# One warp, four feed-forward layers, one core: the written-out issue order of the four compute engines is replaced

## The reference, cut to what matters

```python
x = x + L0_ffn(rigid_transform(x, dx, angle))        # bilinear warp; 1.58-bit FFN, gelu
x = x + L1_ffn(masked_attention_pool(x, types))      # 4 experts of 256-1024-256, top 2 of 4
x = x + L2_ffn(language_adapter(x, language_ids))    # 64-wide adapter, layernorm; 256x256 product
x = x + L3_ffn(category_matrix(x, cat_ids))          # one 256x256 matrix per image; gated FFN, silu
```

## Time and profile before

| quantity | value |
|---|---|
| median of 3 runs | 3265.25 us (3265.25 to 3265.64) |
| the profiled execution | 3265.25 us, span 3263.0 us |
| mean granted TensorE clock | 0.889 of full speed |
| TensorE busy (matmul) | 2813.0 us, 86% |
| VectorE busy | 1916.6 us, 59% |
| ScalarE busy | 1667.7 us, 51% |
| GpSimd busy | 1460.8 us, 45% |

### The profile page before, as it was taken

The page is one execution under the profiler, slowest core; times in us unless marked ns, Lnnn a source line. Parts: engine busy times, 40 slices in busy tenths (PEclk is TensorE's granted clock), DMA queues, the critical chain, the costliest instruction groups (busy, mean ns, idle before and its releaser), DMA issues.

```text
span 3263.0 us, 53348 instructions
## 1 busy us (share of the span) xinstructions
PE 2813.0 (86%) x14652; PEld 2241.1 (69%) x14652; DVE 1916.6 (59%) x5747; ACT 1667.7 (51%) x2786; POOL 1460.8 (45%) x1796
## 2 busy tenths in 40 slices
PE   3028999999999999999999999999999999999996
PEld 2017777777787777777877777777777777877784
DVE  5355765656566556556665665666656565665432
ACT  0024655555565555556645555565555555655442
POOL 0476554445455544444554444445544454551100
PEclk9558998989999898989989898999989899999996
DMA  4222222211222222212222221222222212221110
GB/s 190 59 39 64 55 61 58 57 44 41 58 56 56 59 58 58 44 42 54 58 58 58 58 52 37 56 54 56 61 57 57 45 41 59 54 55 44 41 38 7
DMA packets 207651, 179.37 MB, mean 55 GB/s; under 512 B 122959, under 2 KB 164692, under 8 KB 206164
## 3 DMA queue, kind: packets, MB, share of 16 engines
q1 hardware_dynamic: 172084, 123.84, 14.0%
q0 software_dynamic: 32768, 39.91, 6.7%
q10 hardware_dynamic: 2466, 11.75, 0.9%
HBM read 156.98 MB, written 9.99 MB: 51 GB/s over the span
## 4 chain that ended last, share of the span: by engine, by line
PE 75%; SPq 9%; DVE 3%; issue 3%; POOL 2%; DMA 2%; ACT 2%; ACTq 0%; DVEq 0%; POOLq 0%
PE bank L1211 27%; PE bank L1222 24%; SPq L528 9%; PE bank L1114 5%; PE bank L1120 4%; PE bank L1102 2%; PE bank L1275 2%; POOL w_win L888 2%; PE bank L1108 2%; PE bank L1251 2%; PE bank L1262 2%; DMA c<-w_out 2%; PE bank L1243 1%; PE bank L1163 1%; PE bank L1178 1%
## 5 line engine op out<-in xcount | busy, mean ns | idle before, releaser
L888 POOL DMA_INDIRECT w_win<-in_windows,w_idx x1024 | 1071.4, 1046 | 412.2 <-issue 295.5
L1211 PE MATMUL bank<-c_T,moe_w 128*128 128x256 f32 x4096 | 1045.5, 401 | 0.0
L1222 PE MATMUL bank<-moe_w,moe_hidden_T 128*128 128x256 f32 x4096 | 976.4, 381 | 0.3 <-ACT moe_hidden_T L1042 0.3
L1211 PEld LDWEIGHTS bank<-c_T,moe_w 128*128 128x128 f32 x4096 | 810.2, 202 | 136.7 <-issue 23.8
L1222 PEld LDWEIGHTS bank<-moe_w,moe_hidden_T 128*128 128x128 f32 x4096 | 758.5, 190 | 125.5 <-issue 21.9
L1042 ACT ACTIVATE moe_hidden_T<-bank,moe_b 128x256 f32<-128x256 f32 x1024 | 428.5, 470 | 404.2 <-PE bank L1211 402.6
L640 DVE TENSOR_TENSOR w_prod<-w_win,w_hat 128x72 f32<-128x72 f32 x2048 | 327.2, 229 | 131.5 <-issue 131.2
L895 POOL TENSOR_SCALAR front_stats<-front_stats 128x2 f32<-128x2 f32 x32 | 6.1, 192 | 843.8 <-ACT q_front L980 843.7
L790 DVE SCALAR_TENSOR_TENSOR x_back<-bank,gates,x_back 128x256 f32<-128x256 f32 x256 | 112.0, 479 | 272.8 <-PE bank L1222 272.6
L1243 PE MATMUL bank<-xT_back,adapters 128*64 128x64 f32 x512 | 85.0, 318 | 177.3 <-ACT xT_back L1048 177.3
L1243 PEld LDWEIGHTS bank<-xT_back,adapters 128*64 128x64 f32 x512 | 61.7, 208 | 204.4 <-issue 161.5
(11 more groups left out here) (222 smaller groups left out, 4123.3 us busy)
## 6 DMA issues: line engine op xcount, KB each, us to landing
L_cond_W<-in_L_cond_W SPq DMA_DIRECT2D x128, 256.0 KB, 3.3
adapters<-in_adapter SPq DMA_DIRECT2D x128, 224.0 KB
w_win<-in_windows,w_idx POOLq DMA_INDIRECT x1024
gamma_beta<-in_gamma_beta SPq DMA_DIRECT2D x128, 128.0 KB
moe_w<-in_moe_w ACTq DMA_DIRECT2D x2, 4096.0 KB
x_front<-in_x SPq DMA_DIRECT2D x32, 256.0 KB
c<-w_out SPq DMA_DIRECT2D x512, 16.0 KB
L_cond_b<-in_L_cond_b SPq DMA_DIRECT2D x128, 64.0 KB, 3.0
```

The costliest lines, as they stand in the source:

```text
L888: gp.indirect_dma_start(out=V[par][:, g_ * WLEN:(g_ + 1) * WLEN], out_offset=None, in_=t["windows"], in_offset=bass.IndirectOffsetOnAxis(a ...
L1211: last = te.matmul((H0, H1)[j % 2][:, (i % 2) * QT:(i % 2 + 1) * QT], moe1[:, (e * NDB + d) * F + f * P:(e * NDB + d) * F + (f + 1) * P], ...
L1222: last = te.matmul(Y[:, u * D:(u + 1) * D], hT[:, (i % 4) * QT + u * P:(i % 4) * QT + (u + 1) * P], moe2[:, i * D:(i + 1) * D], start=(f = ...
```

## The change

Only the table `SLOT` changes: no instruction is added or removed, and no semaphore, buffer or DMA. The order in which the four engines issue the steps of a turn is another one. SP's order stays. `coords` moves from VectorE's slot 0 to 28, `hats` to the last four slots of ScalarE, the steps of all other stages are spread anew.

```diff
--- before.py
+++ after.py
@@ -86,32 +86,33 @@
 
 SLOT = {
     "vector": {
-        "coords": (0,),
-        "front": (1, 2, 3, 4, 5, 6, 7, 8, 15, 18, 20, 22, 23, 24, 25, 26, 28, 37, 39, 40, 41, 42, 43, 44, 52, 53, 54,
-                  67, 68, 69, 70, 74, 75, 76, 89, 91, 92, 93, 95, 96, 98, 99, 100, 101, 102, 104, 105, 107),
-        "warp": (9, 10, 11, 21, 29, 33, 45, 56, 57, 58, 59, 62, 63, 64, 65, 66, 79, 80, 83, 84, 86, 87, 88, 90, 94, 97),
-        "back": (12, 13, 14, 16, 17, 19, 27, 30, 31, 32, 34, 35, 36, 46, 47, 48, 49, 50, 51, 55, 61, 71, 72, 73, 77, 78,
-                 81, 82, 103),
-        "experts": (38, 60, 85, 106),
+        "front": (0, 1, 2, 3, 4, 5, 6, 7, 11, 14, 15, 17, 18, 19, 20, 21, 24, 29, 30, 32, 33, 34, 35, 36, 46, 48, 62,
+                  63, 64, 65, 66, 71, 72, 73, 77, 78, 79, 80, 84, 92, 93, 94, 95, 96, 97, 98, 99, 107),
+        "back": (8, 9, 10, 13, 16, 22, 26, 37, 38, 39, 40, 41, 42, 47, 54, 55, 56, 57, 58, 59, 68, 82, 83, 85, 86, 87,
+                 88, 89, 106),
+        "warp": (12, 25, 27, 31, 43, 44, 45, 50, 51, 52, 53, 60, 61, 67, 69, 70, 74, 75, 76, 90, 91, 100, 101, 102, 103,
+                 104),
+        "experts": (23, 49, 81, 105),
+        "coords": (28,),
     },
     "gpsimd": {
-        "front": (0, 9, 15),
-        "gather": (1, 2, 3, 4, 5, 6, 8, 10, 11, 12, 13, 14, 17, 18, 19, 20, 21, 22, 23, 24, 25, 26, 27, 28, 29, 30, 31,
-                   32, 33, 34, 35, 36, 37),
-        "back": (7,),
-        "mask": (16,),
+        "gather": (0, 2, 3, 5, 9, 10, 11, 12, 13, 14, 15, 16, 17, 18, 19, 20, 21, 22, 23, 24, 25, 26, 27, 28, 29, 30,
+                   31, 32, 33, 34, 35, 36, 37),
+        "front": (1, 6, 8),
+        "back": (4,),
+        "mask": (7,),
     },
     "scalar": {
-        "front": (0, 4, 6, 9, 12, 13, 18, 19, 25, 27, 32, 35, 36, 42, 46),
-        "back": (1, 3, 7, 10, 14, 17, 20, 23, 26, 28, 31, 37, 38),
-        "experts": (2, 5, 8, 11, 15, 16, 21, 22, 24, 29, 30, 33, 34, 40, 41, 44),
-        "hats": (39, 43, 45, 47),
+        "front": (0, 5, 6, 10, 13, 14, 18, 21, 23, 25, 30, 32, 34, 37, 43),
+        "back": (1, 2, 11, 15, 20, 22, 24, 27, 29, 33, 36, 39, 42),
+        "experts": (3, 4, 7, 8, 9, 12, 16, 17, 19, 26, 28, 31, 35, 38, 40, 41),
+        "hats": (44, 45, 46, 47),
     },
     "tensor": {
-        "back": (0, 2, 4, 11, 13, 15, 17, 22, 24, 28, 35, 36, 42, 43, 54, 59),
-        "experts": (1, 5, 6, 8, 9, 12, 14, 16, 19, 20, 23, 25, 26, 29, 31, 32, 33, 38, 39, 40, 41, 45, 46, 47, 48, 50,
-                    52, 55, 56, 57, 58, 60, 61, 63),
-        "front": (3, 7, 10, 18, 21, 27, 30, 34, 37, 44, 49, 51, 53, 62, 64),
+        "back": (0, 2, 5, 16, 18, 21, 25, 29, 31, 35, 39, 46, 47, 52, 58, 63),
+        "experts": (1, 3, 4, 7, 9, 10, 11, 13, 14, 15, 17, 20, 23, 24, 26, 27, 28, 33, 37, 38, 41, 42, 43, 44, 45, 51,
+                    53, 54, 55, 56, 57, 59, 60, 61),
+        "front": (6, 8, 12, 19, 22, 30, 32, 34, 36, 40, 48, 49, 50, 62, 64),
     },
 }
 DVE_STEPS, POOL_STEPS, ACT_STEPS = 120, 18, 4
```

## The result

The changed kernel takes 3432.69 us in the median (3430.69 to 3447.45, 4 runs), the kernel before 3265.44 us beside it (3265.25 to 3266.69, 4 runs): a ratio of 1.0521, 95% interval 1.0492 to 1.0551. It is 167 us slower; 151 were forecast (3416 us), and 3433 lies in the range.

What follows compares the result with a forecast made beforehand. TensorE, 86% busy, bounds the kernel, idling at L1243 for the chain down block, store, regroup, b_T0. 3.77 + 1.14 + 0.9 - 0.8 = 5.0 us in 29 turns, 145, plus 6: 3265 to 3416 us; range 3345 to 3455.

Steps and rivals of the forecast that it cites:

- The second down block: TensorE slot 59 to 63: store, regroup and restart start later by two Y blocks and L1192, +3.77 us a turn.
- Context and router: TensorE slots 48 to 50, now adjacent: idle ahead of L1178 and L1186, +1.14 us a turn, bounds 0 and 1.6.
- The first gate/up pair: TensorE slot 31 waits for ScalarE's q1T, now behind the hid block's gelus: +0.9 us a turn, bounds 0 and 1.5.
- The clock: Turn start: L1251, now behind the second hid block, runs at the high clock, -0.8 us a turn, bounds 0 and -1.1.
- The prologue: Turns -1 and 0, without a store: last warp part at slot 104 instead of 97; guess 6 us, bounds 0 and 12.
- The table load: First Silu on ScalarE: the skill's drain of about 1.38 us, up to 40 us in the sum, was left out.
- Only the move counts: Rival: the copies stay hidden, leaving 3.77 - 0.8 = 3.0 us a turn, 3351 us; chance 0.12.
- no earlier rise: Rival: clock's rise keeps its distance from the restart, 5.8 us a turn, 3439 us; inside the forecast's own range, 0.64.
- the clock no longer falls: Rival: every restart runs at the high clock, -0.2 us a turn, 3259 to 3265 us; 0.06 with the no-effect rival.
- the change does nothing: Rival: the store does not hold the regroup and slot 63 costs nothing; 0.06 together with the full-clock rival.
- VectorE comes late: Rival: at the turn's end VectorE is one L643 (1.35 us) behind, 6.4 us a turn, 3456 us; chance 0.15.

Runs made afterwards that it cites:

- e3: Kernel before with only the second down block moved behind the last two Y blocks and L1192, back_out1 behind the fourth combination: 3958.24 us against 3855.00, ratio 1.0276.
- e1: Changed kernel with SP's regroup of the warp issued ahead of the store: 4242.04 us, ratio 1.0986 to the kernel before.
- e2: Kernel before with SP's regroup of the warp issued ahead of the store: 3631.74 us against 3855.00, ratio 0.9414.
- e6: Changed kernel with ScalarE's copy q1T ahead of the gelus of the hid block before it: 4438.96 us; unedited changed kernel beside it 4439.24.
- p3: p2 with expert blocks again between transpose, context and router, and q1T ahead of the gelus: 3581.52 us, ratio 1.0969 to the kernel before.
- e7: Changed kernel with the turn's start on TensorE in the old order, L1252 ahead of the second hid block: 4456.37 us; unedited changed kernel beside it 4439.24.
- p1: Kernel before with a GpSimd memset and wait behind each of a turn's last 21 gathers: 3339.73 us against 3266.51, ratio 1.0223.
- p2: Changed kernel with a GpSimd memset and wait behind each of a turn's last 29 gathers: 3550.55 us, ratio 1.0872 to the kernel before.

## Why the prediction was right, and where its sizes were off

- **The second down block.** Forecast +3.77 a turn. e3 has it alone: 3.56. In the changed kernel the chain behind it keeps its length, and the restart's wait grows as said (11.21 us where some 11.2 were forecast; the mean is 9.9, since at the loop's jump some of it lies ahead of other lines). This term carries some 60% of the loss (3.56 x 29 = 103 us of the 167), and e1 and e2 show from the other side that the store's wait is what ties the regroup to the block.
- **Context and router.** Forecast +1.14, and just outside its upper bound of 1.6: the idle times are to the digit those of the earlier trace rows, 0.46 and 0.68, but from L1173 to the next Y block it is 3.59 us in the mean, where the three groups took 1.92 between other blocks: +1.67. The rest, 0.53, is in the blocks themselves: a block ahead of a gap loses its overlap of 0.16 with the next, two times here, and the two blocks behind the gaps are 0.11 and 0.10 us longer than in the kernel before, where TensorE does not idle ahead of them (durations are modelled):

```profile
1615.77 1.05 PE L1178 MATMUL bank<-mask,x_front 128*128 128x128 f32 x8
...
1618.39 0.95 PE L1186 MATMUL bank<-router,c_T 128*128 128x4 f32 x8
```

The term of the sum was mis-sized: I added the gaps and left the overlaps out, though for the gate/up pair I had counted them.
- **The first gate/up pair.** Forecast +0.9; 28.9 us in 32 waits are 0.90 a turn. What remains of the stretch's +6.48 after 1.67 and the forecast's own 3.77 for the move is 1.04. No run separates this term: e6 was hidden by the stall, and p3 has it together with the copies.
- **The clock.** Forecast -0.8, found -0.67; e7, which undoes it, costs 17 us, 0.6 a turn.
- **The prologue.** A guess of 6 us with bounds 0 and 12; it was 12.2, at the upper bound. The trace shows where it stands, not which step of these turns holds it; no run separates it.
- **The table load.** The row was the better guide. In the changed kernel a load of 1.28 us starts at 1689.54 and its Silu at 1690.84, again 0.02 us after its end, and TensorE waits for VectorE's product (L850) 3.9 us in the whole kernel, as before. By the estimate from the drain in the Trainium skill (ScalarE: Activation LUTs, What ACT_TABLE_LOAD costs) the sum would have been up to 40 us higher; the forecast without it was 17 us too low, and the terms above are larger than that.
- **The rivals.** "Only the move counts" is refuted by the three waits, "no earlier rise" by L1252's median of 379 ns, "the clock no longer falls" by the hid block behind the restart (3.78 us), "the change does nothing" by the time. "VectorE comes late" did not happen: L864 starts 1.08 us behind the down block's start in the turn shown, as before. It was near: VectorE, done with the warp's last part, waits for the last Y block only 0.6 to 0.95 us in the turns of the loop, and one more L643 (1.35 us) would have made it late.

```profile
1629.80 0.88 DVE L791 SCALAR_TENSOR_TENSOR x_back<-bank,gates,x_back 128x256 f32<-128x256 f32 x2 [0.94 <-PE bank L1223]
```

In the sum the forecast was 5.0 us a turn and 6 of prologue; the profiled execution has 6.0 and 12. The mechanism was right and two sizes were low, the copies and the prologue, of which the second was a guess. The upper end of 3460 named with the bounds of the copies comes out of no sum of these terms: with the copies at 1.6 and 1.5 it is 3447, with the prologue at 12 as well 3453. Of the 36 us by which the profiled one lies above the forecast (3452 - 3416), 28 are the turns' missing microsecond and 6 the prologue. Against the median it is 17 too low; that the median is nearer to the forecast than the execution that was divided up is luck, and what makes the 20 us between them isn't shown.

What was wrong is a statement that the prediction did not make but invites: that each term is a price to be had back. p3 took back the copies' two terms and lost them again to VectorE and ScalarE.

**What stays open.** Why the engines stand still in the gathers in three groups and not in the others, and whether it is the chip. That the gap ends about with the run, and that it is longer with the longer run, is what the traces show; that the run causes it was to be shown by p1 and p2, and these met no stall. The kernels with each other's GpSimd table were not run. And the best order found, e2, has no time without the stall.

## What to carry to other kernels

When a transfer waits in a queue behind a store, everything that moves the store's producer later moves the transfer, whatever the transfer itself needs; look at what the queue issues next before you look at the engines. Price a chain from the instruction that starts it, and fill the time behind it with what would otherwise stand ahead. And a wait that is taken away is a gain only if the work that moves up finds its buffers free: in a schedule as full as this one VectorE was due less than a microsecond later.

## What the runs showed of the hardware that was not expected

- The same kernel had a median of 3265 to 3267 us in two groups of runs and of 3726 to 3855 in three others, and the penalty is not a common factor: the changed kernel lost 5.2% to the kernel before in the first, 19.1% in one with the stall. Chip or time is open.
- In the traces with the stall TensorE, VectorE and ScalarE do next to nothing, and SP issues one DMA in 2 to 6 us, for the later part of an unbroken run of GpSimd's indirect gathers, while GpSimd's own rate is if anything higher (36.1 us for 29 gathers against 37.6). The DMA engines moved no more with it than without: 76 GB/s and a DMA share of 0.31 in a window with the stall, 76 and 0.34 in one without.
- After only 1.56 us of idle time in mid turn, a block of 8 matmuls took 3.50 us, at a granted clock of 0.54 (1.00 ahead of the gap). It happened behind 13 of p3's 31 waits of 1.2 to 2.2 us for VectorE; behind the other 18, of 1.2 to 1.6 us, the same block took 1.97 to 2.00 us. A short wait in mid turn can cost more than its length.
